# Queries and keys of an attention kernel: dense transposes and a scatter by DMA in place of transposes of padded tiles, with new orders, lags and banks

## The reference, cut to what is computed

```python
h = _ln(x, ln1_g, ln1_b)
q = (h @ sa_wq + sa_bq).reshape(Bx, Lx, H, HD) * scale      # H = 16 heads, HD = 16
k = (h @ sa_wk + sa_bk).reshape(Bx, Lx, H, HD)
v = (h @ sa_wv + sa_bv).reshape(Bx, Lx, H, HD)
q, k = _apply_rope(q, cos, sin), _apply_rope(k, cos, sin)
x = x + (_attn(q, k, v, causal=True) @ sa_wo + sa_bo)
h = _ln(x, ln2_g, ln2_b)                                    # q from x, k and v from the context y
x = x + (_attn(q2, k2, v2, causal=False) @ ca_wo + ca_bo)
h = _ln(x, ln3_g, ln3_b)
x = x + (gelu(h @ fc1_w + fc1_b) @ fc2_w + fc2_b)           # FF = 1024
...
attn = softmax(ctx @ x.T)                                   # second attention
out = tanh(concat([ctx, attn @ x]) @ trans_W + trans_b) + ...
```

## Time and profile before

| what | value |
|---|---|
| median of 3 runs | 3208.08 us (3207.03 to 3211.53) |
| the profiled execution's own time | 3209.9 us |
| its span | 3208.1 us |
| TensorE | 3098.6 us busy, 97% |
| weight loads | 2640.9 us, 82% |
| VectorE | 2488.9 us, 78% |
| ScalarE | 2214.6 us, 69% |
| GpSimd | 1331.9 us, 42% |
| DMA, hardware queue | 8.2% of 16 engines' span |
| granted TensorE clock, 200 to 3100 us | 1.00 |

### The profile page before, as it was taken

One profiled execution on the slowest core, in us unless ns is written; L12 is line 12 of the kernel. 1 busy time (PEld: TensorE's weight loads), 2 busy tenths in 40 slices (PEclk: granted clock), 3 DMA queues, 4 the chain that ended last, 5 costly groups with the idle time before them and its releaser, 6 DMA issues.

```text
span 3208.1 us, 95131 instructions
## 1 busy us (share of the span) xinstructions
PE 3098.6 (97%) x39884; PEld 2640.9 (82%) x39884; DVE 2488.9 (78%) x5326; ACT 2214.6 (69%) x4737; POOL 1331.9 (42%) x2180
## 2 busy tenths in 40 slices
PE   3799999999999999999999999999999999999997
PEld 2678888888888888888888888888888888888886
DVE  3688788787777877877877887887887878778774
ACT  0367777777777777777777777777777777777775
POOL 0344444444444444444444444444444444444432
PEclk7799999999999999999999999999999999999999
DMA  3000000000000000000000000000000000000000
GB/s 87 22 15 26 24 24 26 24 27 23 23 27 24 22 27 24 22 27 24 22 27 24 22 27 24 22 27 24 24 26 24 27 23 24 27 24 22 27 17 13
DMA packets 103596, 81.50 MB, mean 25 GB/s; under 512 B 32384, under 2 KB 102912, under 8 KB 103168
## 3 DMA queue, kind: packets, MB, share of 16 engines
q1 hardware_dynamic: 103168, 75.41, 8.2%
HBM read 56.49 MB, written 16.78 MB: 23 GB/s over the span
## 4 chain that ended last, share of the span: by engine, by line
PE 79%; DVE 18%; issue 1%; ACT 1%; SPq 1%; DMA 0%; POOL 0%; POOLq 0%; DVEq 0%; ACTq 0%
PE sc L379 14%; PE A L353 7%; PE A L354 6%; PE A L355 6%; PE B L348 5%; PE C L353 5%; PE A L348 4%; PE B L430 4%; PE A L571 4%; PE C L355 4%; PE C L354 4%; PE B L441 3%; DVE rs_kc L724 3%; DVE ot_c L740 3%; DVE ot_s L740 3%; PE B L353 2%
## 5 line engine op out<-in xcount | busy, mean ns | idle before, releaser
L1181 POOL TENSOR_TENSOR kcf<-tkc,rope_c 128x256 f32<-128x256 f32 x128 | 107.4, 839 | 718.7 <-DVE tkc L718 718.7
L1019 ACT ACTIVATE pt_s<-sc 128x512 f32<-128x512 f32 x512 | 264.6, 603 | 88.0 <-PE sc L369 88.0
L353 PE MATMUL A<-h_hi,w_f_hi 128*128 128x256 f32 x1024 | 309.2, 302 | 8.6 <-ACT qtm_s L1012 0.8
L731 DVE TENSOR_REDUCE z_s<-sc 128x8 f32<-128x1024 f32 x256 | 301.7, 1221 | 11.4 <-PE sc L369 5.9
L731 DVE TENSOR_REDUCE z_c<-sc 128x8 f32<-128x1024 f32 x256 | 300.6, 1217 | 0.2
L354 PE MATMUL A<-h_lo,w_f_hi 128*128 128x256 f32 x1024 | 287.6, 281 | 0.0
L355 PE MATMUL A<-h_hi,w_f_lo 128*128 128x256 f32 x1024 | 287.4, 281 | 0.0
L1181 POOL TENSOR_TENSOR qkf<-tqk,rope_c 128x512 f32<-128x512 f32 x128 | 181.0, 1414 | 241.3 <-DVE tqk L715 241.3
L1019 ACT ACTIVATE pt_c<-sc 128x512 f32<-128x512 f32 x512 | 264.6, 603 | 21.7 <-PE sc L379 20.3
L1186 POOL TENSOR_TENSOR rstd<-bmv,eps_t 128x1 f32<-128x1 f32 x384 | 84.8, 221 | 449.0 <-DVE bmv L898 290.6
L718 DVE TENSOR_TENSOR cw<-A,bias_t 128x256 f32<-128x256 f32 x128 | 54.3, 425 | 265.2 <-PE A L578 258.4
(11 more groups left out here) (229 smaller groups left out, 10767.6 us busy)
## 6 DMA issues: line engine op xcount, KB each, us to landing
xt_f<-in_x_t SPq DMA_DIRECT2D x128, 128.0 KB, 2.3
rows_in<-in_x SPq DMA_DIRECT2D x128, 128.0 KB, 2.2
rows_in<-in_ctx_t SPq DMA_DIRECT2D x128, 128.0 KB, 2.2
out<-o_out SPq DMA_DIRECT2D x128, 128.0 KB, 1.7
qtm_s<-zt_s SPq DMA_DIRECT2D x512, 2.0 KB
qtm_c<-zt_c SPq DMA_DIRECT2D x512, 2.0 KB
pt_s<-in_L_xattn_fc_w SPq DMA_DIRECT2D x1, 1024.0 KB, 5.0
rows_in<-in_L_xattn_fc_w SPq DMA_DIRECT2D x1, 1024.0 KB, 5.7
```

Source lines behind the costliest of these rows:

```text
L353: pe.matmul(out, a_hi, b_hi, start=first, stop=False, skip_group_check=True)
L731: dve.tensor_reduce(out, sc[:, 2 * h:2 * h + 2, :].rearrange("p r (g k) -> p r g k", g=G), AX_X, ALU.max, negate=True).then_inc(signal, 1)
L1019: act.activation(pt[c][:, r, :, :].rearrange("p g q -> p (g q)"), sc[:, r, :], ACT.Exp).then_inc(signal, 1)
L1181: pool.tensor_tensor(out[:, :].rearrange("p (h e) -> p h e", e=HD), t[:, :].rearrange("p (h e) -> p h e", e=HD), rope_c[:, :].unsqueeze(1) ...
```

## The change

1. **No padding ahead of the transposes.** `qkz`, `qcz`, `kcz` are gone. `addqk_`, `addqc_`, `addkc_` write a dense tile `qkf` of 512 columns, queries then keys. Four transposes turn both together (`trqk_s_` in A0, `trqk_c_` in B0), eight a tile in place of 16.
2. **ScalarE copies, then begins transfers.** `qks_`/`qkc_` copy the turned tile to a staging tile `qkst`. Then ScalarE itself begins two SBUF-to-SBUF transfers (`spread`) that put its 128 dense rows on the even rows of `qkt` (queries in blocks 0 to 3, keys in 4 to 7). The odd rows of `qkt` hold constants that ten extra transfers load once at the start, and the row of maxima. `qr_s_`/`qr_c_` then round the queries from `qkt` into `qt`. So ScalarE makes four copies of 128x512 in place of six and begins four transfers a tile.
3. The approximate scores use 31 rows (`MX`) where they used 19 and 16. The values lie at a stride of 17 columns in place of 32.
4. **New orders, lags and banks on every engine.** TensorE's lags reach 11 slots where they reached 7; ScalarE, POOL and DVE run 11 extra slots too; SP 13 where it had 9. More buffers for `cw`, `vaug`, `xres_c`. Waits that follow from others are left out or bounded to the first and last tiles.

Core of the diff:

```diff
-MX = HD + NF
+MX = 2 * HD - 1
+VW = HD + 1
...
+        qkf = {c: sb(f"qkf_{c}", [P, 2 * E]) for c in "sc"}
+        qkst = {c: sb(f"qkst_{c}", [P, G, P]) for c in "sc"}
+        qkt = {c: ring(f"qkt_{c}", [P, 2 * G, P], 2) for c in "sc"}
...
+            sp.wait_ge(st_zero, 1)
+            for c in "sc":
+                for b in range(2):
+                    sp.dma_start(qkt[c][b][MX:P:32, G:2 * G, :], d["c_ones"]).then_inc(ld_rows, 16)
+            for b in range(2):
+                for j in range(NF):
+                    sp.dma_start(qkt["s"][b][2 * j + 1:P:32, :, :], d["c_blocks"][j]).then_inc(ld_rows, 16)
...
-                    transposes(A0, qz["s"].rearrange("p h e -> p (h e)"), G).then_inc(s["trq_s"], 1)
-                    transposes(A1, kz["s"].rearrange("p h e -> p (h e)"), G).then_inc(s["trk_s"], 1)
+                    transposes(A0, qkf["s"][:, :], G).then_inc(s["trqk_s"], 1)
+                    transposes(B0, qkf["c"][:, :], G).then_inc(s["trqk_c"], 1)
...
-                    plus(qkz[:, :, 0:HD], per_head(qkf[:, :]), per_head(rs_qk[:, :]), s["addqk"])
+                    plus(qkf["s"][:, :], qkf["s"][:, :], rs_qk[:, :], s["addqk"])
...
+            def qks_(t):
+                if live(t):
+                    copy(qkst["s"][:, :, :], per_k(A0, 2 * E), s["qks"])
+            def qr_s_(t):
+                if live(t):
+                    need(act, dqk_s[t % 2], 32 * (t // 2 + 1))
+                    copy(qt["s"][:, :, :], qkt["s"][t % 2][:, 0:G, :], s["qr_s"])
+            def spread(c, t, landed):
+                for h in range(2):
+                    act.dma_start(qkt[c][t % 2][0:P:2, h::2, :],
+                                 qkst[c][64 * h:64 * h + 64, :, :]).then_inc(landed[t % 2], 16)
+            def dqk_c_(t):
+                if live(t):
+                    need(act, s["qkc"], done(t))
+                    spread("c", t, dqk_c)
...
             def rounded(c, t):
-                pool.tensor_tensor(kr[c][:, :, :], kt[c][t % NB["kt_" + c]][:, :, :],
+                pool.tensor_tensor(kr[c][:, :, :], qkt[c][t % 2][:, G:2 * G, :],
```

More of the change, by code:

```diff
@@ L299, in slot @@
             def slot(u):
-                store_(u - 9)
                 ld_t_(u)
+                store_(u - 13)
+                ld_c_(u - 4)
+                zd_c_(u - 7)
+                zd_s_(u - 4)
                 ld_x_(u)
[L303 to L307, removed]
+            steps(slot, 13)
             for q in st_o:
@@ L460, in qc_ @@
                     need(pe, s["x2t_lo"], done(t))
-                    split3_k(B0[:, 0:E], (x2t_hi, x2t_lo), "cq").then_inc(s["qc"], 1)
-            def trq_c_(t):
-                if live(t):
-                    need(pe, s["ot_s"], done(t + 1))
-                    if t >= TILES - 1:
-                        need(pe, s["addqc"], done(t))
-                    transposes(B0, qcz[:, :, :].rearrange("p h e -> p (h e)"), G).then_inc(s["trq_c"], 1)
+                    split3_k(A1[:, 0:E], (x2t_hi, x2t_lo), "cq").then_inc(s["qc"], 1)
             def p1c_(t):
@@ L631, in _ @@
+                kvc_(u - 4)
+                p1s_(u - 2)
+            steps(slot, 11)
         @block.vector
@@ L833, in x2t_lo_ @@
                     need(dve, s["x2t_hi"], done(t))
-                    minus_hi(x2t_lo[:, :, :], per_k(B0), x2t_hi[:, :, :], s["x2t_lo"])
+                    minus_hi(x2t_lo[:, :, :], per_k(A1), x2t_hi[:, :, :], s["x2t_lo"])
             def tqc_(t):
@@ L999, in slot @@
-                rinv_c_(u - 3)
-                att_c_(u - 3)
-                norm_c_(u - 3)
-                tkc_(u - 2)
-            steps(slot, 7)
+                cw_(u - 6)
+                x1_(u - 5)
+                st3_(u - 8)
+                mv3_(u - 8)
+                rotqk_(u - 2)
+                st2_(u - 5)
+                x2t_lo_(u - 5)
+                ot_c_(u - 7)
+                mv2_(u - 5)
+                rinv_c_(u - 7)
+                att_c_(u - 7)
+                norm_c_(u - 7)
@@ L1007, in _ @@
+                frec_(u - 11)
+                max_s_(u - 3)
+                x2_(u - 7)
+                zt_s_(u - 3)
+                hla_(u - 8)
+                norm_s_(u - 4)
+                rotkc_(u - 5)
+                addqc_(u - 5)
+                addkc_(u - 5)
+                hlb_(u - 8)
+            steps(slot, 11)
         @block.scalar
@@ L1127, in fatt_t_ @@
                     need(act, s["trfa"], done(t))
-                    copy(fatt_t[:, :], B0[:, 0:P], s["fatt_t"])
+                    copy(fatt_t[:, :], A1[:, 0:P], s["fatt_t"])
             def ftan_(t):
@@ L1288, in shape_constants @@
         "c_ident": np.eye(P, dtype=f),
+        "c_ones": np.ones((G, G, P), f),
+        "c_blocks": np.stack([np.broadcast_to(np.stack([(p // 32 == j).astype(f)] * G + [np.where(p // 32 > j, AFTER, 0.0).astype(f)] * G),
+                                              (G, 2 * G, P)) for j in range(NF)]),
         "c_rope_c": np.concatenate([cos, cos], 1),
```

520 lines of the change are left out of this document (247 added, 273 removed).

## The result

The changed kernel takes 3395.91 us (median of 4 runs, 3375.45 to 3408.76) against 3209.04 us before, a ratio of 1.058 (95% interval 1.052 to 1.063). I had forecast 3165 us and a range of 3085 to 3275. The profiled execution took 3375.45 us, its span 3373.7 us; before, the span was 3208.1.

The account below looks back on a forecast made before the run. TensorE was taken to set the slot, with VectorE reaching in; after the change, a ring of 23.4 us through ScalarE, VectorE and TensorE. 3208.1 - 70 + 24 = 3162 us, rounded to 3165; range 3085 to 3275.

Parts of the forecast that it names:

- The bound before, and the transposes: Steps on TensorE setting the 23.98 us slot: eight fewer transposes save 0.88 us a tile, perhaps the 0.34 us hole too.
- the floor: The shortest slot TensorE's own work allows in the changed kernel: 22.8 us, called 22.9 with 0.1 of other waits.
- the ring: Dependent work from the end of `f1b` in one slot to the next, through ScalarE, VectorE and TensorE; forecast's chance 0.35.
- Rival 3: Dense transposes or copies from SBUF dearer than thought: slot loses 0.2 to 0.5 us, 3208 us; chance 0.07 with the rest.
- The begins: Step on ScalarE starting four transfers a tile: 0.5 us each, ScalarE gaining 1.2 us and losing 2.0 a tile.
- Rival 1: Begins on ScalarE cost next to nothing, so the 22.9 us slot holds: 3094 us; chance 0.25.
- The transfers are covered: Step on transfers: a load lands 2.3 us after its begin, wanted much later; even three times as long, nothing would wait.
- rival 2: GpSimd's operations make VectorE's wait (shut-out), `xt_lo` first, 0.75 us a slot: 3260 us with one, 3350 with both; chance 0.33.
- The new ring: Step summing ScalarE 8.5, VectorE 5.6 and TensorE 9.3 to a 23.4 us slot, 0.55 us less than before.
- its dearer form: Besides `xt_lo`, `addqk` and `ct_lo` also meet GpSimd's `fout` and `kr_s`, up to 0.7 us more: 3350 us, outside the range.
- Start and end: Step on ten more initial transfers, 4 to 5 us, and four more TensorE slots, 20 us: together 24, range 5 to 40.
- What would show it: Signs in the later profile: 23.4 us slot, VectorE idle about 2 us before `x2t_lo`, TensorE waits about 0.7 us a slot.

Follow-up runs that it names:

- e_swap: The changed kernel with ScalarE's copy `x2t_hi` moved ahead of the two begins of the cross-attention transfers: 3074.52 us, ratio 0.958 to the kernel before.
- e_sp: The changed kernel with all four begins of the spreading transfers moved from ScalarE to SyncE: 3060.46 us, ratio 0.954 to the kernel before.
- e_best: The changed kernel with begins on SyncE, `xt_lo` and `addqk` ahead of `x2t_lo` on VectorE, `fout` and `kr_s` ahead of `rs2` on GpSimd: 3033.01 us.
- e_double: The changed kernel with two more transfers per tile, into an unread buffer, begun by ScalarE ahead of the real cross-attention ones: 3563.95 us.
- e_nobegin: The changed kernel without its four spreading transfers, their begins and the waits for them; `fout`'s wait for `ftan` stated in every slot: 3153.99 us.
- e_fill: The changed kernel with TensorE's 16 `p1c` matmuls computed three times over, just ahead of the wait for `h_lo`: 3358.39 us.

## Why the prediction was wrong, step by step

- **The bound before, and the transposes**: right, but for the floor. With the begins out of the ring and `addqk` undisturbed the slot of e_swap is 22.83 us and that of e_sp 22.66, against the floor of 22.8 to 22.9 us. With the other edits too it is 22.42 us in e_best, 0.4 us under the floor: TensorE's own work was shorter than I made it, by what no run parts. Rival 3 is out: four dense transposes have a record of 0.60 us in e_swap as four padded ones had the earlier trace rows, the 16 matmuls of 31 rows 0.67 us as those of 19, and the copy from SBUF (`qr_c`) takes 0.64 us, not twice 0.59.
- **The begins**: the step had the right place and too small a price. I took 0.5 us for each and 1.1 us for the two with the wait for the copy. They take 0.60 to 0.62 us each as a rule and now and then up to 1.8 us, and ScalarE's wait at `x2t_hi` is 188.1 / 128 = 1.47 us a slot. That is +0.37 us. Rival 1 is out: e_double shows the price at the end of the kernel.
- **The transfers are covered**: wrong for `qkt_c` in its reason. I wrote that it was wanted "most of a slot later by `kr_c`". In fact begin, landing, `kr_c` and `p1c` of a tile lie in one slot, some 6 us together. In the changed kernel this cost little: `kr_c` waited for the landing 35 times, 29.7 us in all, and as a rule ran right behind `rs2`, as rival 2 had it. In e_swap and e_sp it waits for the landing in every slot, and that decides where it falls among VectorE's operations: against e_sp, e_nobegin measures it at 94 us.
- **The new ring**: right as to its members, wrong in its length, 23.4 us against a slot of 25.19. Its ScalarE part is 0.37 us longer as above. In its VectorE part I had `addqk` at 0.63 to 0.69 us and `ct_lo` at 0.41; they have means of 1.28 and 0.95: +0.59 and +0.54. In its TensorE part the half-clock stretches are (115 - 45) / 128 = +0.55 us, an estimate from the mean clocks of the two spans. 23.4 + 0.37 + 0.59 + 0.54 + 0.55 = 25.45 us, 0.26 more than measured; the terms overlap somewhere by that much, and where is open. Two slips of the recorded sum change little: ScalarE's terms add up to 8.4 us and not 8.5, and 23.98 - 23.4 is 0.58 us and not 0.55.
- **Rival 2** is what came true, at 0.33, in its dearer form (3350 us, which I had left out of the range). Its first victim was wrong: `xt_lo`, at 405 ns, gets in 0.02 us after `kr_c` begins. So the form I gave as likely, one shut-out for 3260 us, did not happen, and the form with `addqk` and `ct_lo`, 1.13 us a slot, did. **This is the step that failed most**: the forecast's sum priced VectorE's part of the ring undisturbed, `addqk` at 0.63 us and `ct_lo` at 0.33, though the text beside it had GpSimd's `rs2`, `kr_c`, `fout` and `kr_s` start from the same `ot_c` in every slot. My argument against it was that `xt_lo` need only get in first. It did, and it saved nothing, since the two operations behind it were caught in its place. Rival 2 already contained the ring (24.2 = 23.4 + 0.75, rounded). That its dearer form came to 3350 us, 46 us short of the result, is part luck: it had 0.75 us for `xt_lo` that did not come, and neither the clock nor the dearer begins.
- **The clock** was in no step. All my prices for TensorE were taken at 1.00, and in this ring 18 of 29 waits of some 2 us had the lower level behind them. That feeds back, since the slower stretch lies on the ring; e_fill, which won 38 us with added work, shows a part of it.
- **Start and end**: 3373.7 - 128 x 25.19 = 149 us against 141 by the same reckoning before, +8 in place of +24.
- **What would show it**: the largest wait of VectorE was to be 2 us a slot at `x2t_lo` (it is 2.6), TensorE's 0.7 us at `h_lo` and `ot_s` (1.35 at `h_lo`, and 0.68 at `x2t_lo`, not named), and a mean of 1.0 in `addqk` was to be rival 2 (1.28).

## What to carry to other kernels

A begin of a transfer is an instruction of 0.6 us on the engine that gives it: put it behind whatever another engine waits for, or on an engine with nothing to compute, and look at everything behind it, not only at the next. When a ring sets the time, add up all that can lengthen it, shut-outs and the clock after a hole included, and do not leave the dear case out of the range because one operation may escape it. A transfer that lands earlier can be worse, if its reader then runs beside an operation of another engine that it shuts out.

## What the runs showed of the hardware that I had not expected

- Begins on ScalarE (those of `qkt_c`) took 597 ns at least and 615 in the middle, up to 1792; SyncE's for the same transfers 628, 655 and 1863.
- GpSimd's and VectorE's operations with two inputs in SBUF shut each other out both ways: beside each other `addqk` takes 1.53 us (0.68 alone), `o_out` 1060 ns on average (729 before), `kr_c` 1295 (1042). `xt_lo`, whose record begins 0.02 us after `kr_c`'s, was not held (0.38 us); there `kr_c` took 1.31 us.
- TensorE was granted 1.2 GHz for some 3 us behind a hole of 2.04 us (with one of 1.10 us 6 us ahead of it), in a kernel that keeps it busy 89% of the time. Of 29 holes of 1.97 to 2.06 us 18 had the lower level behind them, of 37 holes of 1.31 to 1.40 us 6, and in e_nobegin of 43 holes of 1.26 to 1.28 us none. Repeated matmuls put into the hole made the kernel 38 us faster.
